# A column of ones behind each context head makes the token sums part of the Gram product

## What is computed

```
def _channel_attention(qm, km, vm, scale):          # 4 heads of 128 channels
    scores = einsum('bhdn,bhen->bhde', qh, kh) * scale   # sum over the 512 tokens n
    attn = softmax(scores, axis=-1)
    return einsum('bhde,bhen->bhdn', attn, vh)
scale = 512 ** (-0.5)
att = _channel_attention(q*wqg + bqg, k*wkg + bkg, v*wvg + bvg, scale) \
    + _channel_attention(q*wql + bql, k*wkl + bkl, v*wvl + bvl, scale)
x = layernorm(x + 2.0 * att * wp + bp)
```

## Time and profile before

| | us |
|---|---|
| median of 3 runs | 2333.93 |
| the profiled execution | 2335.3 |
| its span | 2333.7 |

### The profile page before, as it was taken

One profiled execution on the slowest core, in us unless ns is written; L12 is line 12 of the kernel. 1 busy time (PEld: TensorE's weight loads), 2 busy tenths in 40 slices (PEclk: granted clock), 3 DMA queues, 4 the chain that ended last, 5 costly groups with the idle time before them and its releaser, 6 DMA issues.

```text
span 2333.7 us, 35377 instructions
## 1 busy us (share of the span) xinstructions
PE 2310.2 (99%) x12382; PEld 1930.7 (83%) x12382; DVE 1695.8 (73%) x3005; ACT 1160.9 (50%) x1926; POOL 427.1 (18%) x356
## 2 busy tenths in 40 slices
PE   9999999999999999999999999999999999999998
PEld 7878887888888888888888888888888888888787
DVE  8976685776778677786777877768777777867643
ACT  5354544554455544645446454554454555554553
POOL 1111211121021211212112021220212102122200
PEclk9999999999999999999999999999999999999999
DMA  9355436476574775757657576675756657464332
GB/s 335 88 165 179 153 132 197 133 222 145 178 204 142 214 181 184 198 129 248 152 200 186 140 251 149 198 198 134 251 132 221 176 166 211 140 201 127 105 115 88
DMA packets 130784, 406.79 MB, mean 174 GB/s; under 512 B 28338, under 2 KB 31538, under 8 KB 120498
## 3 DMA queue, kind: packets, MB, share of 16 engines
q1 hardware_dynamic: 95714, 364.64, 48.3%
q0 software_dynamic: 16896, 33.56, 9.4%
q10 hardware_dynamic: 18000, 6.35, 1.4%
HBM read 377.70 MB, written 26.79 MB: 173 GB/s over the span
## 4 chain that ended last, share of the span: by engine, by line
PE 94%; DVE 2%; issue 2%; ACT 1%; POOL 1%; DMA 0%; SPq 0%; POOLq 0%; DVEq 0%; ACTq 0%
PE acc L1659 28%; PE m L1402 13%; PE h_ps L1635 10%; PE h_ps L1637 9%; PE h_ps L1636 9%; PE m L1432 7%; PE m L1512 2%; PE m L1590 2%; PE m L1495 2%; PE m L1494 2%; PE m L1493 2%; PE m L1616 1%; PE acc L1402 1%; PE m L1470 1%; PE m L1471 1%
## 5 line engine op out<-in xcount | busy, mean ns | idle before, releaser
L742 ACT ACTIVATE hid<-h_ps,b 128x512 f32<-128x512 f32 x252 | 173.6, 689 | 552.2 <-PE h_ps L1637 551.5
L1402 PE MATMUL m<-xT_hi,wq 128*128 128x512 f32 x1320 | 408.3, 390 | 1.1 <-DVE xT_lo L1361 1.1
L1659 PE MATMUL acc<-we_hi,h_hi 128*128 128x512 f32 x1008 | 401.6, 398 | 1.6 <-DVE h_lo L1238 1.6
L1635 PE MATMUL h_ps<-x2T_hi,we_hi 128*128 128x512 f32 x1008 | 399.0, 396 | 2.3 <-DVE x2T_lo L1222 2.3
L1659 PE MATMUL acc<-we_lo,h_hi 128*128 128x512 f32 x1008 | 393.4, 390 | 0.0
L1659 PE MATMUL acc<-we_hi,h_lo 128*128 128x512 f32 x1008 | 393.3, 390 | 0.0
L1636 PE MATMUL h_ps<-x2T_lo,we_hi 128*128 128x512 f32 x1008 | 392.8, 390 | 0.0
L1637 PE MATMUL h_ps<-x2T_hi,we_lo 128*128 128x512 f32 x1008 | 392.8, 390 | 0.0
L1238 DVE TENSOR_TENSOR h_lo<-hid,h_hi 128x512 fp32r<-128x512 f32 x252 | 205.7, 816 | 224.9 <-ACT h_hi L749 224.8
L1228 DVE TENSOR_TENSOR we_lo<-raw,we_hi 128x1024 fp32r<-128x1024 f32 x256 | 332.6, 1299 | 36.0 <-ACT we_hi L732 35.8
L662 ACT ACTIVATE e_f<-m,sb_qkv,scale 128x512 f32<-128x512 f32 x116 | 90.5, 780 | 478.8 <-PE m L1432 476.7
(11 more groups left out here) (301 smaller groups left out, 3568.4 us busy)
## 6 DMA issues: line engine op xcount, KB each, us to landing
raw<-in_w SPq DMA_DIRECT2D x256, 512.0 KB, 4.7
wq<-wq_scratch SPq DMA_DIRECT2D x168, 512.0 KB, 4.2
wp<-wp_scratch SPq DMA_DIRECT2D x77, 512.0 KB, 8.4
x<-in_x_tok SPq DMA_DIRECT2D x16, 1024.0 KB, 11.1
x<-in_b_proj POOLq DMA_DIRECT2D x16, 1024.0 KB, 12.2
ctx_T<-in_ctxT SPq DMA_DIRECT2D x16, 1024.0 KB, 7.6
x<-in_b POOLq DMA_DIRECT2D x16, 1024.0 KB, 11.6
ctx_tok<-in_ctx_tok SPq DMA_DIRECT2D x15, 1024.0 KB, 6.5
```

The costliest lines, as they stand in the source:

```text
L742: act.activation(hid[:, f % 2, :], up_bank(b, f)[:, :], ACT.Relu, bias=b1[:, b % 2, f:f + 1]).then_inc(h_done, 1)
L1402: pe.matmul(bank(a, j)[:, :], w[:, s, t, :], x_hi[:, t, :], start=(t == 0 and s == 0), stop=False)
L1635: pe.matmul(ps, we_hi[:, g % NW, js], x2T_hi[:, j, :], start=(j == 0), stop=False)
L1659: last = pe.matmul(acc[t][:, :], hx[:, f % 2, ts], wx[:, g % NW, C:], start=(f == 0 and n == 0), stop=(f == FC - 1 and n == 2))
```

## The change

In batches 2 to 15:
- `ctx_tok` becomes [128, 4, 4, 129]: each head's 128 channels are followed by one column that GpSimd sets to 1.0 once. The load of the context and all readers and writers of y skip that column. The context load is now made of runs of 128 elements (512 bytes) instead of whole contiguous rows.
- `gram` multiplies by 129 columns. Column 129 of each head's product is then the token sum of x1. Three heads of 129 columns fill 387 columns of `M2`; the fourth goes to `H_PS`.
- `gram` waits until `hidden(b, 0)` has read `H_PS`. `up(b, 1)` waits until ScalarE has copied the sums.
- ScalarE copies the sums in two instructions at the `SCORES` slot, before all other work of that half-step but for an FFN split, after both passes of `scores_inner`.
- `scores_inner` does, for each of its two passes, three heads in one instruction and the fourth in another.
- `x_sums` on TensorE, its copy on ScalarE and the `tile_sum` on GpSimd that fed it are gone.

```diff
+WITH_SUMS = range(2, NB)
-        ctx_tok = sb("ctx_tok", [P, TT, C])
-        y = ctx_tok
+        ctx_tok = sb("ctx_tok", [P, TT, XH, P + 1])
+        y = ctx_tok[:, :, :, 0:P]
...
+        def sums_copied(c):
+            return c + 1 if c < WITH_SUMS.start else 2 * (c + 1) - WITH_SUMS.start
+
+        def gram_out(c, h):
+            if c not in WITH_SUMS:
+                return by_head[:, h, :]
+            return M2[:, h * (P + 1):h * (P + 1) + P + 1] if h < XH - 1 else H_PS[:, 0:P + 1]
...
-                        sp.dma_start(context(a)[:, :, :], d["ctx_tok"][a]).then_inc(ctx_in, 16)
+                        sp.dma_start(context(a)[:, :, :, 0:P], d["ctx_tok"][a].rearrange("p t (h e) -> p t h e", h=XH)).then_inc(ctx_in, 16)
...
+            pool.memset(ctx_tok[:, :, :, P:P + 1], 1.0).then_inc(made, 1)
...
-                    if a > 0:
+                    if a > 0 and a not in WITH_SUMS:
                         tile_sum(a, xsum_done)
...
+                if (c := at(i, h, SCORES)) is not None and c in WITH_SUMS:
+                    act.wait_ge(sc_done, 12 * c + 2)
+                    act.wait_ge(sq_done, 3 * c - 1)
+                    act.activation(s_x[:, 0:XH - 1], M2[:, 0:(XH - 1) * (P + 1)].rearrange("p (h e) -> p h e", h=XH - 1)[:, :, P], ACT.Copy).then_inc(sx_done, 1)
+                    act.activation(s_x[:, XH - 1:XH], H_PS[:, P:P + 1], ACT.Copy).then_inc(sx_done, 1)
...
                 for v, wqv in enumerate((WQG, WQL)):
+                    if c in WITH_SUMS:
+                        some = XH - 1
+                        dve.tensor_tensor(s_a[:, v, 0:some, :], M2[:, 0:some * (P + 1)].rearrange("p (h e) -> p h e", h=some)[:, :, 0:P],
+                                          cols[:, wqv, 0:some].unsqueeze(2).broadcast_to([P, some, P]), ALU.mult)
+                        dve.tensor_scalar(s_a[:, v, some, :], H_PS[:, 0:P], cols[:, wqv, some:XH], None, ALU.mult).then_inc(sc_done, 1)
+                        continue
...
+                if c in WITH_SUMS:
+                    pe.wait_ge(made, MADE + 1)
+                    pe.wait_ge(h_done, FC * (c - 1) + 1)
+                wide = P + 1 if c in WITH_SUMS else P
                 for h in range(XH):
                     hs = slice(h * P, h * P + P)
                     for t in range(TT):
-                        last = pe.matmul(by_head[:, h, :], X[c % NX][:, t, hs], context(c)[:, t, hs], start=(t == 0), stop=(t == TT - 1))
+                        last = pe.matmul(gram_out(c, h), X[c % NX][:, t, hs], context(c)[:, t, h, 0:wide], start=(t == 0), stop=(t == TT - 1))
...
+                if f == 1 and b + 1 in WITH_SUMS:
+                    pe.wait_ge(sx_done, sums_copied(b + 1))
                 ps = up_bank(b, f)[:, :]
...
-                if (c := at(i, h, X_SUM)) is not None:
+                if (c := at(i, h, X_SUM)) is not None and c not in WITH_SUMS:
                     x_sums(c)
```

More of the change, by code:

```diff
@@ L308, in ahead, with tiles, tiles_of_two, quarter_y @@
             return a == 1 and CC * j + t < AHEAD
+        def tiles(x):
+            return x.rearrange("p (t e) -> p t e", e=P)
+        def tiles_of_two(x):
+            return x.rearrange("p k (t e) -> p k t e", e=P)
         def numer(a):
-            return X[NX - 1] if a == 1 else y
+            return X[NX - 1][:, :, :].rearrange("p c (t e) -> p c t e", e=P) if a == 1 else y
+        def quarter_y(a, k, n):
+            return numer(a)[:, 2 * k:2 * k + 2, 2 * n:2 * n + 2, :]
+        def sums_copied(c):
[4 more added lines that the diff above has]
+            return M2[:, h * (P + 1):h * (P + 1) + P + 1] if h < XH - 1 else H_PS[:, 0:P + 1]
         def qk(a):
@@ L322, in context @@
         def context(c):
-            return X[NX - 1] if c == 1 else ctx_tok
+            return X[NX - 1][:, :, :].rearrange("p t (h e) -> p t h e", h=XH) if c == 1 else ctx_tok
         def staged(j):
@@ L604, in mix @@
                     pool.wait_ge(g_mm, c + 1)
-                    pool.wait_ge(xsum_done, (TT - 1) * c)
+                    if c not in WITH_SUMS:
+                        pool.wait_ge(xsum_done, (TT - 1) * c)
                     for t in range(TT):
@@ L613, in mix @@
                     pool.wait_ge(x2_done, TT * c + TT)
-                    pool.wait_ge(sx_mm, c + 1)
+                    if c in WITH_SUMS:
+                        pool.wait_ge(mean_mm, c)
+                    else:
+                        pool.wait_ge(sx_mm, c + 1)
                     if c > 0:
@@ L690, in high_block @@
                     act.wait_ge(y_done, CC * a + (2 if b == A11 else 4))
-                    raw_b = quarter(numer(a), *{A11: (0, 0), A12: (1, 0), A22: (1, 1)}[b])
+                    raw_b = quarter_y(a, *{A11: (0, 0), A12: (1, 0), A22: (1, 1)}[b])
                 else:
                     act.wait_ge(sum_done, 4 * k + {S3: 1, S1: 2, S2: 3, S4: 4}[b])
-                    raw_b = raw_sum(b)
-                act.activation(piece(a, b, 0), raw_b, ACT.Copy).then_inc(yhi_done, 1)
+                    raw_b = tiles_of_two(raw_sum(b))
+                act.activation(tiles_of_two(piece(a, b, 0)), raw_b, ACT.Copy).then_inc(yhi_done, 1)
             def prepare(i, h):
@@ L979, in combine @@
                     dve.wait_ge(q_mm, CC * a + CC)
-                    one, two, op = quarter(y_a, 0, 0), quarter(y_a, 0, 1), ALU.subtract
+                    one, two, op = quarter_y(a, 0, 0), quarter_y(a, 0, 1), ALU.subtract
                 if b == S1:
                     dve.wait_ge(y_done, CC * a + 4)
-                    one, two, op = quarter(y_a, 0, 1), quarter(y_a, 1, 1), ALU.add
+                    one, two, op = quarter_y(a, 0, 1), quarter_y(a, 1, 1), ALU.add
                 if b == S2:
                     dve.wait_ge(sum_done, 4 * before(a) + 2)
-                    one, two, op = raw_sum(S1), quarter(y_a, 0, 0), ALU.subtract
+                    one, two, op = tiles_of_two(raw_sum(S1)), quarter_y(a, 0, 0), ALU.subtract
                 if b == S4:
                     dve.wait_ge(sum_done, 4 * before(a) + 3)
-                    one, two, op = quarter(y_a, 1, 0), raw_sum(S2), ALU.subtract
-                dve.tensor_tensor(raw_sum(b), one, two, op).then_inc(sum_done, 1)
+                    one, two, op = quarter_y(a, 1, 0), tiles_of_two(raw_sum(S2)), ALU.subtract
+                dve.tensor_tensor(tiles_of_two(raw_sum(b)), one, two, op).then_inc(sum_done, 1)
             def low_block(a, b):
@@ L1133, in token_sums @@
             def token_sums(c):
-                dve.wait_ge(sx_done, c + 1)
+                dve.wait_ge(sx_done, sums_copied(c))
                 dve.tensor_tensor(s_q[:, 0, :], s_x[:, :], cols[:, WQG, :], ALU.mult).then_inc(sq_done, 1)
@@ L1561, in attention_T @@
                 pe.wait_ge(asum_done, c + 1)
-                pe.wait_ge(sx_done, c + 1)
+                pe.wait_ge(sx_done, sums_copied(c))
                 for h in range(XH):
```

16 lines of the change are left out of this document (8 added, 8 removed).

## The result

The changed kernel takes 2386.78 us (median of 6 runs, 2382.88 to 2393.75), the kernel before beside it 2333.82 (6 runs, 2332.51 to 2338.97). The ratio is 1.0223, with an interval of 1.0212 to 1.0234: 53 us slower, where 45 were forecast. The profiled execution of after took 2382.9 us with a span of 2381.2, so it shows 47.5 us of the 53; it was the fastest of the six runs, and their median lies 4 us above it. One execution of the run swap_to14 (3870 us) and one of the kernel before (9204 us) stand far from all others and are left out of the ratios.

A forecast was written before the change was run, and what follows sets the result against it. The prediction took TensorE's queue, busy 99% of the span, as the bound. From 2333.9 us, waits and saving (-8.3 + 1.05 + 36.7 + 2.75 = +32.2) and the clock (+13) gave 2379 us, range 2361 to 2394.

The forecast's parts named there:

- rival 4: x_sums ran in the shadow of its neighbours, so its 8.3 us aren't saved: 2387 us; chance counted with the forecast.
- x_sums: Removing this step from TensorE's queue saves 0.595 us a batch, -8.3 us over 14 batches.
- The wider product: gram's 129th column on each of 32 matmuls was taken as 0, at most 0.4 us in all.
- rival 3: The Gram product becomes slower by its layout, 2428 us if gram doubles; a doubled context load belongs here too; 10%.
- Gram's wait in batch 15: gram waits 0.94 us for hidden(b, 0) to read H_PS, plus 0.11 for the restart: +1.05 us.
- The stall of up(b, 1): TensorE waits 2.95 us for scores_inner and the copies, plus 0.11 restart, in 12 batches: +36.7 us.
- Batch 15 and batch 2: Ahead of up(b, 1): a 2.64 us stall in batch 15, +2.75 with restart; 0 in batch 2, at worst 0.9.
- The clock: TensorE's clock falls behind some of 13 stalls, between 0 and 22 us; 8 falls of 1.6 us taken, +13 us.
- every one: Sign of being wrong: a clock that is 1.00 or 0.50 behind every one of the stalls.
- Rival 1: The stalls of TensorE come but the clock doesn't fall: 2366 us; 25%.
- Rival 2: Ahead of up(b, 1), VectorE's chain fits in TensorE's 4.55 us, no stall comes, only x_sums goes: 2326 us; 5%.

The follow-up runs named there:

- swap_to14: The changed kernel with scores_inner moved ahead of the projections' work on VectorE, new sums only in batches 2 to 14: 2330.26 us, ratio 0.9985.
- no_sums: The kernel before without tile sum, x_sums and its copy in batches 2 to 15, reusing batch 1's token sums: 2324.94 us, ratio 0.9960.
- wait_only: The kernel before with one added wait: up(b, 1) waits for both passes of scores_inner in batches 2 to 15: 2388.06 us, ratio 1.0230.
- busy: The changed kernel with 12 dummy products on TensorE where it waits ahead of up(b, 1): 2371.97 us, ratio 1.0162.
- early: The changed kernel with the fourth head read and copied first, up(b, 1) waiting for that copy alone: 2366.56 us, ratio 1.0141.
- swap: The changed kernel with scores_inner moved ahead of the projections' work on VectorE in batches 2 to 15: 2331.64 us, ratio 0.9989.
- layout: The changed kernel with the new sums in no batch, only the wide ctx_tok and its load in 512-byte runs: 2334.59 us, ratio 1.0003.
- swap_early: The changed kernel with scores_inner ahead of the projections' work and H_PS given back earlier, in batches 2 to 15: 2329.62 us, ratio 0.9978.
- busy8: The changed kernel with 8 dummy products on TensorE where it waits ahead of up(b, 1): 2371.85 us, ratio 1.0158.
- best: The changed kernel with scores_inner ahead of the projections' work, H_PS given back earlier, new sums only in batches 2 to 14: 2328.75 us, ratio 0.9978.

## Why the prediction was right

Forecast 2379 us, measured 2386.78, inside the range of 2361 to 2394. The mechanism is the one that was forecast, a chain through VectorE and ScalarE that gives H_PS back too late, and a clock that falls behind the stalls; how often it falls was not known from any row, and there the forecast was low. The measured number is also rival 4's, 2387, so the number alone doesn't decide between them; no_sums and the profile do.

- **x_sums, -8.3.** no_sums: about -9. Right.
- **The wider product, 0.** gram takes 3.48 us from its first matmul to the down's first (1158.74 to 1162.22), 109 ns for each of 32. Three heads and one head together cost what four did. Right, and rival 3 is out: gram is not slower, and layout costs nothing (ratio 1.0003). The Trainium skill, "PSUM — Partial Sum Buffer", section "Specifications (TRN2)", has cachelines of 8 bytes and slower matmuls for non-contiguous patterns. The trace agrees as far as it goes: these patterns are contiguous, and the head at column 129, which starts off such a line, costs nothing more. That a weight load's time doesn't go by the moving operand was the prediction's own reading of the formula in the Trainium skill, in which that operand isn't named; the 109 ns with 128 and with 129 columns bear it out here.
- **Gram's wait in batch 15, 0.94 + 0.11.** A gap of 0.87 us, which is 1.03 from start to start. Right.
- **The stall of up(b, 1), 12 times 2.95 + 0.11.** The start is 3.05 us late, so about 3.15 with the restart: 1.1 us too little over 12 batches. What VectorE does ahead of scores_inner was priced exactly (5.68 us from 1163.20, against 5.67 in the earlier trace rows); the 0.1 lies behind it. From scores_inner's start to TensorE's release it is 1.93 us (1168.88 to 1170.81), not 1.83. The narrow VectorE instruction, priced by the earlier trace rows at 0.28 us and 0.20 from start to start, is 0.34 and 0.26 (1169.33 to 1169.59), twice: VectorE needs 1.52 us instead of 1.42. The two copies overlap almost fully, 0.07 us apart, and give 0.09 back, but TensorE starts 0.14 us behind the second copy's end (1170.67) and not 0.05.
- **Batch 15 and batch 2.** 2.59 us against 2.64; none against none. Right, and in batch 2 for the reason given: the scans take 1.22 and 1.20 us in after and in no_sums, where the tile sum is gone, and 1.52 and 2.23 us in before and wait_only, where GpSimd's tile sum runs beside them.
- **The clock, 8 falls of 1.6 = 13.** This is the mis-sized term: 12 falls of 1.53 us, 18.4, and 16.7 net of the one that went. The cause was named (gaps as in batch 0), its count was a guess between 0 and 13: it took two thirds, and expected windows below 1.00 behind about half of the stalls. They stand behind 12 of 13, one short of the "every one" that it had named as a sign of being wrong; that the range held the number in spite of it is owed to its upper end, which allowed for all 13. busy shows that it is the idle time of TensorE and not the lateness of up that brings them: the same lateness with dummies in the gap has none of the 12. Rival 1 (2366, no fall) is ruled out by the windows behind the stalls. The prediction took it also from the Trainium skill, "TensorE: Matmul & The Clock Gate", section "Part 1: The HAM clock gate (the "warmup" mystery)", by which an idle window brings the lower clock. Read as the prediction read it, that rule doesn't hold here: single gaps of 2.9 us in dense work were followed by the lower clock 12 times of 12, and even gaps of 1.9 us 6 times of 12. The Trainium skill also calls its window free-running. That could fit the like gaps with different ends in early, but no run here shows it.
- **Rival 2 (faster)** needed the chain to fit into the cover. It didn't in after, by 3.05 us; in swap it nearly does, and the ratio is 0.9989. The rival's place was right, and its missing piece was the order of VectorE.
- **Rival 4** is out by no_sums.

In the spans the forecast's +45.2 us are 2.3 short of the 47.5 measured: 3.7 us of clock and 1.1 of stalls too little, against 2.3 us of waits of before that are gone and that it didn't foresee (1.6 and 0.7, below). The remaining 5.5 us of the miss are the difference between the profiled execution and the runs.

What the forecast's sum doesn't hold, and what remains of the 53 us: a wait of 1.6 us (acc for h_lo) and a slow stretch near 370 us are in the profile of before and not in that of after. The slow stretch begins at a gap in which TensorE waits for `rden_all`, and that gap is 2.49 us in before and 1.74 in after. TensorE and the window, before and then after:

```profile
372.53 1.22 PE L1456 MATMUL m<-rden_all,head_all 128*128 128x512 f32 x2 [2.49 <-ACT rden_all L831]
...
370.00:375.00 5.00, 2.51 (x7) 0.71 1.10 228
```

```profile
370.97 0.72 PE L1489 MATMUL m<-rden_all,head_all 128*128 128x512 f32 x2 [1.74 <-ACT rden_all L859]
...
370.00:375.00 5.00, 4.03 (x24) 1.00 1.11 236
```

Both come and go with small shifts of the schedule (layout has the wait of 1.6 us, no_sums has not), so 2 to 3 us of any single profiled execution belong to neither theory. In busy, the same accounting leaves 1 to 2 us of the span without a place. And the 4 us by which the runs of after lie above their profiled execution, with a spread of 11 us against 6 before, are open; a number of falls that differs between executions would do it. early's two kinds of gaps suggest it, and so does swap_early, whose profiled execution was the slowest of its ten and shows 5.1 us of work lost. It was not measured.

## What to carry to other kernels

When a buffer is borrowed from another step, the price is set by the reader that gives it back: look at what is queued on that engine ahead of the read, here three unrelated instructions of 3 us, and move the read ahead of them before you count the saving. A stall of TensorE in an otherwise dense kernel can cost half as much again through the clock (2.9 us of gap, 1.5 us of slow work behind it); where a gap can't be avoided, work in it, or making it as short as 1 us with no other gap near, kept the clock here. And a step that is removed is worth its distance of starts on the bounding engine, 0.6 us a batch, so a single new wait of more than that per batch undoes it.

## What the runs showed of the hardware

How often TensorE's clock fell to its lower level behind a gap in the middle batches, each gap with dense matmuls around it; batch 15's gap is left out, and told beside it:

| kernel | gap us | falls |
|---|---|---|
| busy | none, filled with dummies | 0 of 12 |
| busy8 | 1.0 | 0 of 12 |
| early | 1.9 | 6 of 12 |
| wait_only | 2.4 | 11 of 12 |
| after | 2.9 | 12 of 12 |

In batch 15 the clock fell in wait_only (gap 2.07 us), but not in after and swap (2.6), nor in early and swap_early (1.6). Near 370 us, where TensorE waits for `rden_all`, it fell in the six kernels whose gap was 1.96 to 3.44 us (before, layout, busy, busy8, early, swap_early) and in none of the six whose gap was 1.74 to 1.78 us (after, swap, swap_to14, best, wait_only, no_sums). Behind the pair of 1.25 and 0.87 us in batch 15 it fell in three of six. Each fall in the table cost 1.5 to 1.7 us of work in the 5 us behind it. I had taken the chance of a fall at about 60% for gaps of 2.95 us, and had not expected gaps of like length to differ in it. GpSimd's tile sum slowed VectorE's scans beside it in batch 2 from 1.20 to 2.23 us. The last surprise is small: two copies of a few elements on ScalarE, each recorded as 0.17 us, start 0.07 us apart, so the second costs next to nothing, while a VectorE instruction on 128 columns of PSUM (TENSOR_SCALAR) costs 0.26 us from start to start where one on 384 (TENSOR_TENSOR) costs 0.45 to 0.47.
